# The front stages of the next image beside the stream of attention units, in two fixed places of every chunk

## What is computed

```
x = x + window_attention(group_norm(x))     # 16 heads of 8; each pixel against its 7x7 window, with a bias
t = tokens(x)                               # 3136 tokens of 128
t = t + attention(layer_norm(t))            # 8 heads of 16, all tokens against all
t = t + layer_norm(t) @ w_lora.T @ W.T      # w_lora from 4-bit codes and scales
```

## Time and profile before

| | |
|---|---|
| time, median of 3 runs | 10139.77 us |
| the profiled execution: its time, its span | 10123.25 us, 10121.2 us |
| granted clock of TensorE, mean | 0.928 |
| PE busy | 8905.5 us, 88% of the span |
| DVE busy | 7995.4 us, 79% |
| ACT busy | 6473.8 us, 64% |
| POOL busy | 1653.8 us, 16% |
| DMA | 276.39 MB, mean 27 GB/s |

### The profile page before, as it was taken

One profiled execution on the slowest core, in us unless ns is written; L12 is line 12 of the kernel. 1 busy time (PEld: TensorE's weight loads), 2 busy tenths in 40 slices (PEclk: granted clock), 3 DMA queues, 4 the chain that ended last, 5 costly groups with the idle time before them and its releaser, 6 DMA issues.

```text
span 10121.2 us, 420263 instructions
## 1 busy us (share of the span) xinstructions
PE 8905.5 (88%) x166082; PEld 4676.6 (46%) x166082; DVE 7995.4 (79%) x13637; ACT 6473.8 (64%) x13361; POOL 1653.8 (16%) x1701
## 2 busy tenths in 40 slices
PE   6799977999779996799977999679997799977999
PEld 5344453444534445344453444534445344463444
DVE  6799767997679966799667996679966799667996
ACT  3388834888348883488834888348883488834887
POOL 5100051000510005100051000510005100060000
PEclk9799987999879998799987999879998799987999
DMA  4300043000430004300043000430004300042000
GB/s 74 59 3 3 3 70 57 3 3 3 71 56 3 3 3 71 55 3 3 3 73 53 3 3 3 74 52 3 3 3 74 52 3 3 3 77 50 3 3 9
DMA packets 386621, 276.39 MB, mean 27 GB/s; under 512 B 49836, under 2 KB 377244, under 8 KB 383516
## 3 DMA queue, kind: packets, MB, share of 16 engines
q1 hardware_dynamic: 378524, 229.58, 13.9%
q0 software_dynamic: 6144, 19.28, 1.2%
HBM read 144.03 MB, written 25.86 MB: 17 GB/s over the span
## 4 chain that ended last, share of the span: by engine, by line
PE 78%; issue 11%; DVE 3%; SPq 3%; ACT 2%; DMA 1%; POOL 1%; ACTq 0%; DVEq 0%; POOLq 0%
PE PS L666 21%; PE PS L729 20%; PE PS L707 20%; PE PS L590 4%; PE PS L601 4%; PE PS L612 3%; SPq L400 2%; DVE block_max L1094 2%; ACT arena L898 1%; PE PS L635 1%; PE PS L697 1%; PE PS L693 1%; PE PS L639 1%; PE PS L561 1%; PE PS L630 1%
## 5 line engine op out<-in xcount | busy, mean ns | idle before, releaser
L1062 DVE TENSOR_REDUCE block_max<-PS 128x1 f32<-128x448 f32 x10192 | 5691.1, 618 | 489.0 <-PE PS L666 361.8
L898 ACT ACTIVATE arena<-PS 128x448 f32<-128x448 f32 (+1 forms) x11200 | 5259.7, 559 | 1158.5 <-PE PS L729 1133.4
L666 PE MATMUL PS<-KP,arena 96*32 96x448 bf16 x43904 | 4107.3, 372 | 359.0 <-DMA KP<-arena 282.1
L729 PE MATMUL PS<-arena,KP 99*32 99x448 bf16 x43904 | 3997.1, 354 | 110.5 <-ACT arena L898 75.7
L707 PE MATMUL PS<-arena 128*32 128x448 f32 x22400 | 2631.3, 539 | 19.3 <-ACT arena L898 14.9
L666 PEld LDWEIGHTS PS<-KP,arena 96*32 96x32 bf16 x43904 | 1233.3, 98 | 2084.9 <-issue 544.9
L729 PEld LDWEIGHTS PS<-arena,KP 99*32 99x32 bf16 x43904 | 1227.4, 96 | 1684.4 <-ACT arena L898 905.6
L827 ACT ACTIVATE arena<-PS 80x512 f32<-80x512 f32 (+1 forms) x896 | 428.8, 538 | 1036.7 <-PE PS L601 1035.7
L513 POOL CAST shift_parts<-shift 14x128 bf16<-14x128 f32 x112 | 31.5, 281 | 5427.7 <-ACT shift L864 5427.7
L707 PEld LDWEIGHTS PS<-arena 128*32 128x32 f32 x22400 | 681.4, 110 | 385.7 <-ACT arena L898 90.6
L986 DVE TENSOR_TENSOR arena<-PS,nat_bias 128x80 f32<-128x80 f32 (+3 forms) x1120 | 354.1, 383 | 498.6 <-PE PS L590 498.4
(11 more groups left out here) (97 smaller groups left out, 4382.3 us busy)
## 6 DMA issues: line engine op xcount, KB each, us to landing
arena<-vT_padded SPq DMA_DIRECT2D x1792, 70.0 KB
arena<-arena SPq DMA_DIRECT2D x384, 98.0 KB, 4.3
KP<-arena POOLq DMA_DIRECT2D x192, 98.0 KB, 8.1
KP<-arena SPq DMA_DIRECT2D x192, 98.0 KB, 4.4
arena<-in_x SPq DMA_DIRECT2D x9, 1568.0 KB, 6.5
vT_padded<-arena SPq DMA_DIRECT2D x16, 784.0 KB
out_y<-X SPq DMA_DIRECT2D x56, 224.0 KB, 2.4
arena<-shift_parts SPq DMA_DIRECT2D x336, 3.5 KB
```

Of the source, the lines that this page charges most:

```text
L666: ins = mm(PS[at:at + QT, bank, 0:BLK], QP[0:ROWS, g, unit_queries(unit, h, t, QT)], KP[0:ROWS, g, h, j * BLK:(j + 1) * BLK], start=True, ...
L729: ins = mm(PS[k0:k0 + 32, at % banks, 0:BLK], KP[0:ROWSM, g, h, c * P + k0:c * P + k0 + 32], QP[0:ROWSM, g, unit_queries(unit, h)], start= ...
L898: nc.scalar.activation(exp_buffer(c)[0:n, h, :], PS[0:n, bank, 0:BLK], ACT.Exp, scale=float(ADIM) ** -0.5).then_inc(exp_done, 1)
L1062: V.tensor_reduce(block_max[:, q, j:j + 1], PS[:, max_banks()[0][m][0], 0:BLK], AX.X, ALU.max).then_inc(max_read, 1)
```

## The change

- The stages 1 to 3 of image b+1 no longer stand in front of its stream. They are cut into pieces, and class `Plan` gives each a slot beside image b's units: a chunk (numbered 0 to 349) and one of two places in it. On PE these are behind the first and the third score group of the chunk; the other engines do the tasks of a slot between their own work of the chunk. Image 0 does the same list by itself ahead of everything (`alone`), with eight banks in turn.
- A strip takes 9 chunks (`PERIOD`): its score pieces, maxima, subtraction, exponentials, sums, transposes and values each have their slot, and so have block stages, norm and ffn (`tails`). Slots that are taken push a piece to the next.
- Each PE piece writes bank 7 (`SIDE_BANK`); before it, PE waits until the piece before was read. Maxima have banks 3, 4, 5 alone.
- All fourteen units have maxima of a later one beside them, across the images too. The last norm and ffn of a block stand in the first half of the unit behind its projection.
- Buffers no longer share a region. Window scores have two buffers (four before), values and transposed weights one (two before), k, q, v and blocks of the front one or two. 448-column matmuls of side pieces are four of 32 columns (`across`).
- The parts of q and k are cut by POOL, by block, and go with v through DRAM (`q_dram`, `k_dram`, `v_dram`). SP loads q by unit two units ahead, k and v by group, all in slot order with window loads, stores, the copy of x into X and the sending of maxima. POOL issues no DMA.
- The loop is four copies: first image, middle (a loop), last (no front), and what is left after it.

```diff
+    def tails(self, attention):
+        units = {"first": range(1, AUNITS), "after": range(1)}.get(attention, range(AUNITS))
+        for k in units:
+            t = k * CHUNKS
+            self.fix(t + 1, 1, "spread", k)
+            self.fix(t + 2, 0, "invert", k)
+            self.fix(t + 2, 1, "normalise_unit", k)
+            self.fix(t + 3, 1, "project", k)
+            if k == 0 or k > NBLK:
+                i = (k - 1 - NBLK) % NBLK
+                self.fix(t + 5, 1, "mean3", i)
+                self.fix(t + 6, 0, "square3", i)
+                self.fix(t + 7, 1, "var3", i)
+                self.fix(t + 9, 0, "scale3", i)
+                self.fix(t + 10, 1, "ffn", i)
+                self.fix(t + 12, 0, "store_out", i)
...
+    def front(self):
...
+        for s in range(STRIPS):
+            t = FIRST_STRIP + PERIOD * s
+            for n in range(3):
+                self.fix(t + n, 0, "scores", 3 * s + n)
+            self.fix(t + 3, 0, "maxima", s)
+            self.fix(t + 4, 0, "subtract", s)
+            self.fix(t + 5, 1, "exponentials", s)
+            self.fix(t + 6, 0, "sum_up", s)
+            self.fix(t + 8, 0, "invert_strip", s)
+            self.fix(t + 8, 1, "normalise", s)
+            for c in range(4):
+                self.fix(t + PERIOD + 3 + c, 0, "turn", 4 * s + c)
+            self.fix(t + 2 * PERIOD - 1, 0, "values", s)
+            self.fix(t - 4, 0, "spread_queries", s)
+            self.fix(t + (PERIOD if s else 0), 0, "load_windows", s)
+        self.place(22, "gn_mean", 0)
...
+            t = FIRST_STRIP + PERIOD * BLOCK_STRIPS * j - 7
+            self.fix(t, 1, "norm", NBLK + j)
+            self.place(t + 1, "q1", j)
+            t = FIRST_STRIP + PERIOD * (BLOCK_STRIPS * (j + 1) + 1)
+            t = self.place(t, "proj", j)
+            t = self.place(t + 1, "mean2", j)
+            self.fix(t + 1, 0, "square2", j)
+            t = self.place(t + 2, "var2", j)
+            self.fix(t + 2, 0, "scale2", j)
+            t = self.place(t + 3, "k2", j)
+            self.fix(t + 1, 0, "split_k", j)
+            self.fix(t + 3, 0, "store_k", j)
+            t = self.place(t + 1, "q2", j)
+            self.fix(t + 2, 0, "split_q", j)
+            t = self.place(t + 1, "v2", j)
+            self.fix(t + 1, 1, "store_v2", j)
+            self.fix(t + 4, 0, "store_q", j)
+        self.fix(t + 4, 1, "load_k", 0)
+        self.fix(t + 4, 1, "load_v", 0)
+
...
+        def each_image(eng, image):
+
+            image(0, "first")
+            if images > 2:
+                with eng.Fori(1, images - 1) as b:
+                    image(b, "middle")
+            image(images - 1, "last")
+            image(images, "after")
...
+                def load_windows(s):
+                    row = window_row(s)
+                    wait(sp, vT_out, of(b, ahead, 32 * NBLK, 32 * ((row + WI - 1) // BLOCK_ROWS + 1)))
+                    wait(sp, pv_in, of(b, ahead, STRIPS, s))
...
+                def load_q(k):
+                    g, i = divmod(k % AUNITS, NBLK)
+                    wait(sp, q_out, of(b, k // AUNITS, 16 * NBLK, 16 * (i + 1)))
+                    wait(sp, queries_of_unit, of(b, 0, AUNITS * 96, k * 96))
+                    wait(sp, st_ready, of(b, 0, AUNITS * GH * CHUNKS, (last_user(k) + 1) * (GH * CHUNKS)))
...
+            def across(bank, weights, rhs, n=BLK):
+
+                for at in range(0, P, 32):
+                    ins = mm(PS[at:at + 32, bank, 0:n], weights[:, at:at + 32], rhs, start=True, stop=True,
+                             tile_position=(0, at))
+                return ins
...
+                def beside(t, sub):
+                    if (t, sub) in plan.taken:
+                        pe.wait_ge(*side_read(b, 1, *previous[0]))
+                        apart(pe)
+                        do(*plan.taken[t, sub], SIDE_BANK)
+                        previous[0] = plan.taken[t, sub]
...
                         for h in range(GH):
-                            scores_turned(c, h)
-                            if h == weigh_at and c > 0:
-                                weigh(unit, c - 1)
-                            if h == weigh_at and c == 0 and before is not None:
-                                weigh(before, CHUNKS - 1)
+                            scores_turned(k, c, h)
+                            if h == 0:
+                                beside(k * CHUNKS + c, 0)
+                            if h == 2 and c > 0:
+                                weigh(k, c - 1)
+                            if h == 2 and c == 0 and (k > 0 or kind != "first"):
+                                weigh(k - 1, CHUNKS - 1)
+                            if h == 2:
+                                beside(k * CHUNKS + c, 1)
                             maxima(1)
                         maxima(len(steps))
```

More of the change, by code:

```diff
@@ L72 @@
 FIRST_STEPS = max_steps(0).start
[L75 to L86, removed]
 MAX_PIECES = [(0, 2), (2, 4), (4, NBLK)]
@@ L270, in apart, with wait, of @@
+        def wait(eng, s, value):
+            if not isinstance(value, int) or value > 0:
+                eng.wait_ge(s, value)
+            if eng is nc.sync and not isinstance(value, int):
+                apart(eng)
         def apart(eng):
             eng.sem_inc(paced, 1)
+        def of(b, ahead, per, at):
+            return b * per + (ahead * per + at)
         def blk(t, j):
             return t[:, j * BLK:(j + 1) * BLK]
-        def unit_index(b, unit):
-            g, i = unit
-            return b * AUNITS + (g * NBLK + i)
@@ new lines, in hybrid_block, with alone_bank @@
+        alone = Plan(True, None)
+        plans = {name: Plan(name in ("first", "middle"), name) for name in ("first", "middle", "last", "after")}
+        ALONE_SLOTS = max(t for t, sub in alone.at) + 1
+        def alone_bank(task, i):
+            return alone.order.index((task, i)) % 8
+        def each_image(eng, image):
[5 more added lines that the diff above has]
+            image(images, "after")
@@ new lines, in _, with image @@
+            do = side(0, 0)
+            for t in range(ALONE_SLOTS):
+                for sub in range(2):
+                    for task, i in alone.at[t, sub]:
+                        do(task, i)
+            do("load_k", 1)
+            do("load_v", 1)
+            do("load_q", 0)
+            do("load_q", 1)
+            do("send_shift", 0)
+            def image(b, kind):
+                do = side(b, 1)
+                for t in range(AUNITS * CHUNKS):
+                    for sub in range(2):
+                        for task, i in plans[kind].at[t, sub]:
+                            do(task, i)
@@ new lines, in side, with image @@
+                return do
+            do = side(0, 0)
+            for t in range(ALONE_SLOTS):
+                for sub in range(2):
+                    for task, i in alone.at[t, sub]:
+                        do(task, i)
+            do("split_max", 0)
+            def image(b, kind):
+                do = side(b, 1)
+                for t in range(AUNITS * CHUNKS):
+                    for sub in range(2):
+                        for task, i in plans[kind].at[t, sub]:
+                            do(task, i)
@@ L542, in _ @@
+            each_image(pool, image)
         @block.tensor
@@ L791, in _ @@
-                wait_freed(pe, b, FFN, NBLK - 1)
+            each_image(pe, image)
         @block.scalar
```

1541 lines of the change are left out of this document (901 added, 640 removed).

## The result

The changed kernel takes 9904.69 us (median of 4 runs, 9896.01 to 9909.64), the kernel before 10137.89 beside it: a ratio of 0.977 with a 95% interval of 0.975 to 0.979. The forecast was 9300. The direction is right and the time lies in the range given, but of the forecast gain of 840 us only some 230 came.

A forecast was written before the change was run, and what follows sets the result against it. PE and DVE were taken to bound the stream, with idle stages to be folded in. Start 508, seven images of 1130, last image 865 gave 9283 us, plus 2 and 17 for measuring: 9300 us, range 8800 to 9950.

The forecast's parts named there:

- What bounds the kernel; what the change can win: PE and DVE fill the stream; 427 us an image of stages where both wait get folded into it.
- The work of PE (1041 us): PE's work for one image: stream 843, less 8 for small tiles, plus 206 for the front's matmuls.
- T: Time of one image in the new stream: 1100 for PE plus 30 for stalls, 1130 us.
- Switching of the array (59 us): In the stream, each of a strip's seven score and transpose pieces costs PE 0.30 us, 28 strips an image.
- The stalls (30 us): DVE's lumps in each strip exceed PE's lead of some 1.16 us, costing 30 us an image; bounds 0 and 100.
- rival B: In the stream, PE idles 42.2 us at "issue" plus 35 for late send_shift; T 1210, total 9860; chance 0.25.
- Rival C: PE stops at side pieces until the single bank is read; at 0.5 us a piece total 10,534; chance 0.10.
- Late send_shift: At a unit's start, send_shift queued behind window loads is up to 7 us late; hidden in forecast, 35 in the rival.
- Start of the stream: Image 0's front alone, from setup to first maxima, ends at 508 us, bounds 430 to 620.
- the last image: The stream without a front, then last unit, norm, ffn and tail: 783 + 46 + 16 + 20 = 865 us.
- The chances: Whole kernel: faster by over 0.5% 0.87, within 0.5% 0.03, slower 0.10.
- The likeliest case: One image takes 1090 to 1170 us in the stream; chance 0.45.

The follow-up runs named there:

- x3_early_reads: Changed kernel with ScalarE reading the spread sums and transposed maxima half a chunk earlier, in the place in which PE makes them; 9751.19 us, 0.961 of the kernel before.
- x9_all_three: Changed kernel with early ScalarE reads, half of each maximum left out and most bytes of the loads beside the stream left out; 9352.28 us, 0.924 of before.
- x11_lumps: x8_spread_k_early with a strip's maxima and sums each cut into two reductions and the values' fold moved later; 9607.99 us, 0.949 of before.
- x12_all_real: x8_spread_k_early with both the earlier query loads of x10_q_first and the cut reductions of x11_lumps; 9577.1 us, 0.947 of before.
- x10_q_first: x8_spread_k_early with queries of units 0 and 1 loaded right behind group 0's keys in the front that runs alone; 9609.7 us, 0.950 of before.
- x8_spread_k_early: Changed kernel with ScalarE's early reads, keys loaded in three parts far apart and values at other slots; 9650.69 us, 0.953 of the kernel before.
- x2_tiny_windows: Changed kernel with nine tenths of the window loads' bytes left out, same instructions and semaphores; 9814.19 us, 0.967 of the kernel before.

## Why the prediction was off, step by step

**What bounds the kernel; what the change can win.** Right. The 427 us of stages in the earlier trace rows are folded in, PE stays the longest engine, DVE has 973 us of work an image (forecast 980), ACT 808 (809), POOL 225 (250; row 3030 to 4233 us).

**The work of PE (1041 us).** Right: with DMA and late reads gone and maxima halved, T came to 1127. PE's busy time there is 1151.3 of 1203 us, 1079 in an image of 1127, against 1041 + 33 for switching = 1074. The idle time still in it is 50 of 1203 us (22.4 "issue", 20.6 side pieces, 6.7 stream), 47 an image.

**Switching of the array (59 us).** Right in kind; as an addition to the times of the earlier trace rows nearly twice too large. The trace of x3_early_reads has it cleanest:

```profile
3401.59 0.36 PE L1005 MATMUL PS<-QP,KP 99*32 99x448 bf16 x4
3401.89 0.90 PE L815 MATMUL PS<-Kn,QB 32*32 32x80 f32 x40
3402.71 0.37 PE L943 MATMUL PS<-KP,QP 96*32 96x448 bf16 x4
...
3414.97 0.36 PE L1005 MATMUL PS<-QP,KP 99*32 99x448 bf16 x4
3415.26 0.63 PE L824 MATMUL PS<-C,SC 128*80 128x128 f32 x4
3415.82 0.37 PE L943 MATMUL PS<-KP,QP 96*32 96x448 bf16 x4
...
3417.92 0.36 PE L1005 MATMUL PS<-QP,KP 99*32 99x448 bf16 x4
3418.22 0.42 PE L824 MATMUL PS<-C,SC 128*80 128x128 f32 x2
3418.57 0.37 PE L943 MATMUL PS<-KP,QP 96*32 96x448 bf16 x4
```

A group takes 0.19 us, so the score piece costs 3402.71 - 3401.59 - 0.19 = 0.93 us, against 40 x 2.14 / 112 = 0.76 by the earlier trace rows; four transposes cost 0.66 against 4 x 1.73 / 14 = 0.49. Both are 0.17 more, 196 x 0.17 = 33 us an image. That is what the sum lacked, not what a piece costs by itself: the 2.14 and 1.73 of the earlier trace rows run to the end of the last matmul, and so have one such end in them already. Two transposes cost 3418.57 - 3417.92 - 0.19 = 0.46 us, so two more take 0.20, and 0.26 of a piece doesn't depend on its size; the strip's third score piece (32 records, 0.80 us) gives 0.28 in the same way. So 0.30 a piece was nearly right, and the sum counted part of it twice. The Trainium skill (TensorEngine Tiling (Array Packing), Key Properties) says that a change of tiling mode drains the engine. The trace agrees that each piece pays, 0.26 to 0.28 us.

**The stalls (30 us): the step that failed.** 1202.7 less 1074 (1041 and 33 for switching) leaves 129 us where the sum had only the 30 for DVE's lumps. Shown by taking each away: traffic 31, side reads by ACT 22, DVE 19, and these add (x9_all_three). Of the other 57, 47 are the idle time that x9_all_three still has, and 10 are in no row.

- *Traffic, 31 us, put at nothing.* The forecast set rival B's half aside because "in the old stream PE lost nothing to it". The old stream had nothing to lose to: DMA is at 0.01 there, and at 0.49 in the strips, where the 42.2 us of "issue" stand. After the change DMA is at 0.20 throughout, and 43 us of "issue" came along. Both rows were at hand, and the second was read as a property of the strips. That they are waits for instructions, which the forecast left open for L612, the queue q8 shows for both kernels: 33 gaps of 0.4 us or more in the old strips (1302 to 1558 us) end 1.19 to 1.77 us after one of its packets has landed, as the 24 in the new stream do. The Trainium skill (Runtime: NRT & Kernel Launch, Instruction fetch mechanics) says that the sequencer fetches the next page by its own DMA queue while it executes the current one, and that the cost of passing from page to page is mostly hidden. The trace agrees where DMA is at 0.04 (no "issue" in the last image's stream), and not beside the loads: 43 us an image, 18 with most bytes left out.
- *Side reads, 22 us, put at nothing.* Rival C named the mechanism and its place (one bank, readers strictly in order) and gave it all or nothing. It was there at 0.14 us a piece. That most pieces are a chunk apart holds for the average piece, not for two that share a chunk with a read due half a chunk later.
- *DVE.* 19 us or more against 30: about the right size. The mechanism given for it (lumps over a lead) isn't borne out: with the lumps cut, x11_lumps and x12_all_real got back 4 us.

**Late send_shift (B's other half).** Not seen in the stream: the one wait of PE on a DMA is 4.1 us for `shift_parts`, at the first unit of image 0. B's T (1210) is nearly the measured one by luck: its 42 us for "issue" came true, its 35 for a late unit start did not, and the 48 us of waits at side pieces, which it left out, made up for that.

**Start of the stream: 605 us, forecast 508.** The second failed step, 97 of the 611 us by which the span missed (T has 7 x 73 = 509, the last image 5: 870 against 865). Setup and first projections took 92 (105 forecast), strips with their block chains and the last block 398 (341 in the same terms), and then come 53 us in which PE is idle and DMA at 1.03 (row 490 to 545), for which the forecast had only what its 25 for "last block, stores and loads" left; the maxima 62, as forecast. The forecast took the load of k for covered by seven chunks of the stream, which image 0 doesn't have, and didn't ask what stands in the queue ahead of the first queries. Loading those earlier moved the first sums by 24 us (x10_q_first against x8_spread_k_early) and 30 (x12_all_real against x11_lumps). Why the strips alone take 13.2 us each with their chains (28 maxima from 95.97 to 452.49 us) where 11.3 were forecast stays open; less window traffic doesn't help (x2_tiny_windows, first sums at 656.0).

**The chances.** 0.87 for faster is borne out. The likeliest case was too good because each stall was weighed as a rival of its own, present or absent, with the central sum taking only one; parts of three of them together make the loss. That 9904.69 still lies in the range is owed to its width, which B set.

## What to carry to other kernels

- When stages with idle engines are folded under a full one, their idle time is not all won: ask which of their stalls belongs to the place (waiting for a neighbour) and which to the work (DMA bytes, a single buffer's readers). The second kind comes along. A row "issue" in a stretch with heavy DMA and none in a stretch without it is such a stall; the packets of the instruction queue beside its gaps tell whether the engine waited for instructions.
- Small stalls of several kinds add. Put a part of each into the central sum, and keep rivals for sizes that would turn the sign.
- With one shared buffer for side pieces, place each read in the order of its engine directly behind its piece; two lines of the plan gave 22 us an image. In a prologue, load what the first stage reads first.

## What the runs showed of the hardware

- PE stops between matmuls that wait for nothing in the program while large loads run: 43 us an image at a DMA share of 0.20, up to 7.2 us at once with DMA at 1.08; with most bytes gone 18 us, at most 3.3. Each gap of 0.4 us or more ends 1.2 to 1.9 us after a packet of 16 KB of the instruction queue has landed, and in the longest no such packet had started for 18 us. Spreading the same bytes shortened the longest gap to 3.8 us and left 36 us.
- After a gap of 2.4 us PE was granted the lower clock for a stretch (1.71 us for eight matmuls, not 0.93), so a gap can cost more than its length.
- A piece of 32x32 or 128x80 tiles between 96x32 groups costs 0.26 to 0.28 us beyond its streaming, near the 0.30 of an untiled projection in the old stream.
